# A graph layer on one core: the last pieces' x half of W1 is computed at the start, and VectorE adds it back late

## The chip, the cores and the metric

The kernel runs on one core of a Trainium2 chip. The metric is the device time of one execution in microseconds (us). The launch has one core, so nothing else shares its engines.

## The reference

A graph with 6250 nodes and 106250 edges, 128 numbers (f32) for each. `dst`, sorted, names the node that each edge ends in.

```python
agg = segment_sum(edge_attr, dst, num_segments=6250)       # 6250 x 128
h   = concatenate([x, agg, u[0] for every node], axis=1)   # 6250 x 272
h   = relu(h @ W1 + b1)                                    # 6250 x 256
out = h @ W2 + b2
y   = x + (out + x)
return (y - mean(y)) / sqrt(var(y) + 1e-5)                 # over the 128 columns
```

## The kernel before

**Groups and batches.** The edges are cut into 70 groups of 1536 (the last has 266). A group is four windows of 384 edges, and the destinations of a window span fewer than 32 nodes. SyncE loads the groups in order into a ring of 12 slots, 768 KB each (`load_group`, line 276). Two groups make a batch up to group 59; from group 60 on each group is a batch by itself. There are 40 batches; number 30 is the first single one (`late_step`).

For each batch b the engines do this. VectorE compares the local destinations with 0..31 and so makes the one-hot matrices (`make_onehot`, line 594) and a 128-wide placing matrix (`make_place`, lines 603 and 608). TensorE multiplies edges by one-hots (`sum_batch`, line 845), which gives sums by node. ScalarE copies these out of PSUM (`copy_batch`, line 441). TensorE turns and places them (`turn_batch`, line 867), and VectorE adds them to the turned table `agg_t` (`add_batch`, line 630). Step b of TensorE is `sum_batch(b)`, then `turn_batch(b - 1)`, then work on pieces.

**Pieces.** The nodes are cut into ten pieces of 512 (0 to 9, the last of them `LAST`) and the late ones A, B, C_ of 256, D, E of 128 and REST of 106. A piece n can go on once all groups up to `complete_at[n]` are added. Its work: x is turned on TensorE (`turn_x`, line 882) and copied by ScalarE (line 453); `sum_hidden_x` (line 900) multiplies it by the x rows of W1, and `sum_hidden_a` (line 907) adds `agg_t` times the other rows in the same PSUM bank; ScalarE applies bias and Relu (`relu`, line 466); `sum_out` (line 920) multiplies by W2; VectorE forms y and its moments (`moments`: lines 641, 647, 652), ScalarE takes the root (`root`, line 473), and VectorE normalizes (`normalize`: lines 656, 660). GpSimd adds half of b2 to x beforehand (line 402).

**The start.** SyncE loads part of `dst`, group 0, the rest of `dst`, then the groups, with the x of a piece after every sixth group; the late pieces' x stands between groups 53 and 54 (lines 296 to 303). VectorE makes local destinations, TensorE turns them (line 834), ScalarE copies them (line 429). Only then can the first one-hots be made.

**The end.** The order on each engine from batch 30 on is written out by hand. On VectorE it is the following, where `step(b)` is one-hots for batch b + 2, placing for b + 1, then the add of batch b - 1:

```python
            b = late_step
            step(b)
            step(b + 1)
            moments(LAST)
            step(b + 2)
            normalize(LAST)
            step(b + 3)
            moments(A)
```

On TensorE it is `sum_batch`, `turn_batch` of the batch before, and then `sum_out(LAST)` at step 30; hidden A at 31; out A and hidden x of B at 32; hidden a of B at 33; out B at 34; hidden x of C_ at 35; hidden x of D and hidden a of C_ at 36; out C_ and hidden a of D at 37; out D and hidden x of E at 38; hidden x of REST at 39; at last hidden a of E and REST and their outs.

Of the kernel before, what the change touches and what calls it, by code (L numbers as in the profile page):

```python
# [13 lines left out]
R = 3  # L14
# [8 lines left out]
BUFFERS = 3  # L23
# [5 lines left out]
GEN_TILES = 10  # L29


def gnn_resnorm_kernel(nc: bass.Bass, x: bass.AP, dst: bass.AP, edges: bass.AP, u: bass.AP,
# [16 lines left out]
    rest_rows, rest_tiles = divmod(rest_edges, R)  # L49
    agg_cols = (n_nodes // BLOCK + 1) * BLOCK  # L50
    assert 0 < rest_edges <= EDGES_WIN and 0 < rest_tiles and rest_rows < ROWS
# [20 lines left out]
    complete_at = [6, 12, 18, 24, 30, 36, 40, 46, 52, 58, 60, 63, 66, 67, 69, n_grp]  # L72
    assert len(complete_at) == n_pieces
    steady = 6
    assert all(complete_at[n] * BLOCK == pieces[n + 1][0] * IT for n in range(steady))
    late_groups = [(complete_at[n], pieces[n + 1][0]) for n in range(steady, n_pieces - 1)]


    single0 = 60
# [7 lines left out]
    hidden_step = [batch_first.index(complete_at[n]) for n in range(n_big)]  # L87
    out_step = [b + 1 for b in hidden_step]
    turn_x_step = [1] + out_step[:n_big - 1]

    x_parts = [(n,) for n in range(n_big)] + [(A, B), (C_, D, E), (REST,)]
    x_load_at = {1: 0} | {IT * n: n for n in range(1, n_big)}
    x_late_at = 53
# [7 lines left out]
    with ExitStack() as ctx:  # L103
# [27 lines left out]
        late_base = sb("late_base", [P, len(late_groups)])  # L131
# [20 lines left out]
        x_t_late = sb("x_t_late", [P, n_nodes - late0])  # L152
        hid_t = sb("hid_t", [P, 2, m_chunks, BLOCK])
# [25 lines left out]

        def out_bank(n):  # L180
            return xt_ps if n >= n_big and n % 2 == 0 else out_ps
# [3 lines left out]
        bases_landed = sem("bases_landed")  # L185
        weights_landed = sem("weights_landed")
# [26 lines left out]
        x_t_ready = sem("x_t_ready")  # L213
        hidden_summed = sem("hidden_summed")
# [35 lines left out]
        n_weights = 7  # L250
# [6 lines left out]
        CHECK0 = 2  # L257
        WORST_STEP = CHECK0 + 4
        assert out_step[0] < WORST_STEP < out_step[1]

# [5 lines left out]
        def _(sp):  # L266
            dst_full = dst[0:full_grp * EDGES_GRP].rearrange("(g c e) -> g c e", c=C, e=EDGES_WIN)
            sp.dma_start(dst_rows[0:64], dst_full[0:64]).then_inc(dst_landed, 16)

            def load_group(g):  # L270
# [9 lines left out]
                src = edges[g * EDGES_GRP:g * EDGES_GRP + rest_rows * R, :].rearrange("(p r) f -> p (r f)", r=R)  # L280
                to = edge_ring[0:rest_rows, slot, 0:R].rearrange("p r f -> p (r f)")
# [3 lines left out]
                sp.dma_start(edge_ring[rest_rows:rest_rows + 1, slot, 0:rest_tiles],  # L285
# [3 lines left out]
            def load_x(n):  # L289
                node0, p, j = pieces[n]  # L290
                sp.dma_start(rows(n, x_all).rearrange("p j f -> p (j f)"),  # L291
                             x[node0:node0 + p * j, :].rearrange("(p j) f -> p (j f)", j=j)
                             ).then_inc(x_landed[n], 16)

            def load_x_late():
                sp.dma_start(x_all[:, x_slot[A]:x_slot[D]].rearrange("p (n j) f -> p n (j f)", j=J // 2),
                             x[late0:rest0 - 2 * P, :].rearrange("(n p j) f -> p n (j f)", p=P, j=J // 2)
                             ).then_inc(x_landed[n_big], 16)
                sp.dma_start(x_all[:, x_slot[D]:x_slot[REST]],
                             x[rest0 - 2 * P:rest0, :].rearrange("(n p) f -> p n f", p=P)  # L300
                             ).then_inc(x_landed[n_big + 1], 16)
                for r0, r1 in ((0, rest_cut), (rest_cut, rest_nodes)):
                    sp.dma_start(x_all[r0:r1, x_slot[REST]], x[rest0 + r0:rest0 + r1, :]
                                 ).then_inc(x_landed[n_big + 2], 16)

            load_group(0)

            sp.wait_ge(pad_set, 1)
            sp.dma_start(dst_rows[64:full_grp], dst_full[64:full_grp]).then_inc(dst_landed, 16)
            sp.dma_start(dst_rows[full_grp:n_grp, 0, 0:rest_edges],  # L310
                         dst[full_grp * EDGES_GRP:n_edges].rearrange("(o e) -> o e", o=1)).then_inc(dst_landed, 16)
            for g in range(1, n_grp):
# [3 lines left out]
                if g == x_late_at:  # L316
                    load_x_late()
# [88 lines left out]
        def _(act):  # L406
            nc.scalar.preload_act_table(ACT.Sqrt)
            loads = [
                (w1_x[:], w1[0:d, :]),
# [7 lines left out]
            assert len(loads) == n_weights  # L417
            act.dma_start(base_row[0:1, 0:n_grp],
                          dst.rearrange("(o e) -> o e", o=1)[:, 0:n_edges:EDGES_GRP],
                          allow_slow_non_contiguous=True).then_inc(bases_landed, 16)  # L420
            for to, src in loads:
                act.dma_start(to, src, allow_slow_non_contiguous=True).then_inc(weights_landed, 16)

# [8 lines left out]
            last.then_inc(local_t_ready, 1)  # L432

            def copy_batch(b):
# [5 lines left out]
                w = C * WIN if b < n_batch - 1 else WIN  # L440
# [3 lines left out]
            def copy_x_t(k):  # L444
                act.wait_ge(x_turned, k + 1)
                if 2 <= k < n_big:

                    act.wait_ge(hidden_summed, m_chunks * (k - 1))
                at = 0
                for n in x_parts[k]:  # L450
                    node0, p, j = pieces[n]
                    to = x_t[:, k % 2] if k < n_big else x_t_late[:, node0 - late0:node0 - late0 + p * j]
                    last = nc.scalar.copy(to.rearrange("f (p j) -> f j p", j=j),  # L453
                                          xt_ps[:, at:at + p * j].rearrange("f (j p) -> f j p", j=j))
                    at += p * j
                last.then_inc(x_t_ready, 1)

            def relu(n):
                _, p, j = pieces[n]
                for m in range(m_chunks):  # L460

                    act.wait_ge(hidden_summed, m_chunks * n + (m + 1 if n < n_big else m_chunks))
                    if n >= 2 and m == 0:

                        act.wait_ge(out_summed, n - 1)
                    nc.scalar.activation(hid_t[:, n % 2, m, 0:p * j].rearrange("h (j p) -> h j p", j=j),  # L466
# [598 lines left out]
```

## Time and profile before

| | |
|---|---|
| median of 3 runs | 185.4 us (185.38 to 186.12) |
| profiled execution: its own time | 185.73 us |
| profiled execution: span, first to last instruction | 184.0 us |
| TensorE busy | 154.1 us, 84% |
| VectorE busy | 115.4 us, 63% |
| ScalarE busy | 51.5 us, 28% |
| GpSimd busy | 25.4 us, 14% |
| moved | 62.07 MB |

The span is cut into stages by what ends the waits: the stretch until the last pair of groups has landed, the stretch in which the single groups and late pieces are worked off, and the tail of the last piece. An engine's share over the whole span doesn't say which of them it bounds.

### The profile page before, as it was taken

Reading aid. Unit: us, or ns where it says so; the run is one execution under the profiler, and the core shown is the slowest. Engines: PE = TensorE matmul, PEld = TensorE weight load, DVE = VectorE, ACT = ScalarE, POOL = GpSimd, SP = SyncE. Lnnn points to the kernel's source line nnn. Section 1 sums busy time; section 2 is a strip of 40 time slices with the busy share of each in tenths; the row PEclk is TensorE's granted clock in tenths of the full one; section 3 lists DMA queues with packets and bytes.
Section 4 is the critical chain, followed back from the end, with each engine's and each line's share of the span. In section 5 each row is a group of like instructions: output and inputs, shape, how many; then the busy total and the mean of one; then the engine's idle time right before and its main releaser. Section 6 shows DMA issues by size and latency. Waiting matters only on the chain.

```text
span 184.0 us, 5378 instructions
## 1 busy us (share of the span) xinstructions
PE 154.1 (84%) x2195; PEld 113.9 (62%) x2195; DVE 115.4 (63%) x369; ACT 51.5 (28%) x110; POOL 25.4 (14%) x29
## 2 busy tenths in 40 slices
PE   0056979979979979969979999899889799899970
PEld 0046855955955956845846858467458568677850
DVE  6847499568376385485495466954933745877371
ACT  2021233223323313313313343133133241233230
POOL 7800030110200200200200204002003230000000
PEclk9999999999999999999999999999999999999997
DMA  5999999999999999999999999999999999998011
GB/s 119 315 352 373 374 375 373 371 373 374 374 374 373 375 372 373 376 372 373 374 373 374 375 373 374 375 373 360 363 374 374 371 374 370 367 398 303 11 43 33
DMA packets 42196, 62.07 MB, mean 337 GB/s; under 512 B 1975, under 2 KB 39541, under 8 KB 42170
## 3 DMA queue, kind: packets, MB, share of 16 engines
q1 hardware_dynamic: 41046, 61.23, 95.0%
q10 hardware_dynamic: 1124, 0.48, 1.2%
q8 instruction: 18, 0.29, 0.7%
q14 instruction: 8, 0.07, 0.1%
HBM read 58.50 MB, written 3.20 MB: 335 GB/s over the span
## 4 chain that ended last, share of the span: by engine, by line
PE 44%; DMA 39%; SPq 8%; DVE 4%; ACT 1%; issue 1%; DVEq 0%
DMA edge_ring<-in_edge_attr_dram 37%; PE sum_ps L845 17%; PE turn_ps L867 7%; PE hid_ps L907 6%; PE hid_ps L900 6%; PE out_ps L920 5%; SPq L276 4%; SPq L291 3%; DMA base_row<-in_dst_dram 2%; DVE bases L568 2%; PE xt_ps L920 1%; PE xt_ps L882 1%; DVE local_rows L576 1%; ACT local_t L429 1%; PE xt_ps L834 1%
## 5 line engine op out<-in xcount | busy, mean ns | idle before, releaser
L845 PE MATMUL sum_ps<-edge_ring,onehot 128*32 128x128 f32 x1662 | 58.5, 284 | 13.0 <-DMA edge_ring<-in_edge_attr_dram 10.8
L845 PEld LDWEIGHTS sum_ps<-edge_ring,onehot 128*32 128x32 f32 x1662 | 45.2, 113 | 27.9 <-DMA edge_ring<-in_edge_attr_dram 13.3
L630 DVE TENSOR_TENSOR agg_t<-agg_t,turn_ps 128x128 f32 x70 | 20.2, 288 | 56.7 <-PE turn_ps L867 52.6
L594 DVE TENSOR_TENSOR onehot<-iota,local_t 128x768 f32<-128x768 f32 (+1 forms) x40 | 33.6, 843 | 3.0 <-ACT local_t L429 2.4
L402 POOL TENSOR_TENSOR x_all<-x_all,half_b 128x512 f32<-128x512 f32 (+3 forms) x16 | 17.7, 1115 | 127.4 <-PE xt_ps L882 127.4
L466 ACT ACTIVATE hid_t<-hid_ps,bias 128x512 f32<-128x512 f32 (+3 forms) x32 | 18.1, 584 | 37.1 <-PE hid_ps L907 37.1
L867 PE MATMUL turn_ps<-place,sums 128*128 128x128 f32 (+1 forms) x140 | 26.5, 306 | 0.0
L907 PE MATMUL hid_ps<-agg_t,w_a 128*128 128x512 f32 (+3 forms) x64 | 24.1, 500 | 0.6 <-DVE agg_t L630 0.5
L867 PEld LDWEIGHTS turn_ps<-place,sums 128*128 128x128 f32 (+1 forms) x140 | 18.9, 192 | 8.0 <-issue 7.9
L920 PE MATMUL out_ps<-w_sb,hid_t 128*128 128x128 f32 (+1 forms) x176 | 21.9, 275 | 0.0
L441 ACT COPY sums<-sum_ps 128x256 f32<-128x256 f32 (+2 forms) x40 | 13.6, 341 | 25.9 <-PE sum_ps L845 25.9
L920 PEld LDWEIGHTS out_ps<-w_sb,hid_t 128*128 128x128 f32 (+1 forms) x176 | 20.7, 192 | 0.2 <-ACT hid_t L466 0.2
L900 PE MATMUL hid_ps<-x_t,w_x 128*128 128x512 f32 x40 | 18.9, 594 | 0.0
L907 PEld LDWEIGHTS hid_ps<-agg_t,w_a 128*128 128x128 f32 x64 | 11.2, 190 | 11.3 <-issue 6.4
L453 ACT COPY x_t<-xt_ps 128x512 f32<-128x512 f32 x10 | 11.6, 1158 | 22.4 <-PE xt_ps L882 22.4
L660 DVE TENSOR_SCALAR x_all<-x_all,mean_var,rstd 128x128 f32<-128x128 f32 (+1 forms) x49 | 13.9, 342 | 0.5
L608 DVE TENSOR_TENSOR place<-iota,rel_cols 128x256 f32<-128x256 f32 x30 | 13.6, 454 | 0.0
L473 ACT ACTIVATE std<-mean_var,eps_col 128x4 f32<-128x4 f32 (+3 forms) x16 | 4.6, 294 | 27.5 <-DVE mean_var L652 27.5
L647 DVE BATCH_NORM_STATS2 stats<-x_all 128x6 f32<-128x128 f32 (+1 forms) x49 | 11.0, 281 | 0.5
L900 PEld LDWEIGHTS hid_ps<-x_t,w_x 128*128 128x128 f32 x40 | 6.8, 191 | 4.8 <-issue 4.8
L641 DVE SCALAR_TENSOR_TENSOR x_all<-x_all,out_ps 128x512 f32<-128x512 f32 (+3 forms) x13 | 7.8, 599 | 0.4 <-PE out_ps L920 0.4
L826 PE MATMUL out_ps<-ident,rel 70*4 70x70 f32 x1 | 0.3, 277 | 9.1 <-DVE rel L574 9.1
(64 smaller groups left out, 73.0 us busy)
## 6 DMA issues: line engine op xcount, KB each, us to landing
edge_ring<-in_edge_attr_dram SPq DMA_DIRECT2D x69, 768.0 KB, 12.1
x_all<-in_x_dram SPq DMA_DIRECT2D x10, 256.0 KB, 10.5
out_dram<-x_all SPq DMA_DIRECT2D x1, 2304.0 KB
dst_rows<-in_dst_dram SPq DMA_DIRECT2D x1, 384.0 KB
x_all<-in_x_dram SPq DMA_DIRECT2D x1, 384.0 KB, 11.1
out_dram<-x_all SPq DMA_DIRECT2D x3, 128.0 KB
out_dram<-x_all SPq DMA_DIRECT2D x1, 256.0 KB
w_x<-in_L_gnn_W_dram ACTq DMA_DIRECT2D x1, 128.0 KB, 5.9
```

The source lines that it names most:

```text
L402: nc.gpsimd.tensor_tensor(xn, xn, half_b2[0:p].unsqueeze(1).broadcast_to([p, j, d]), ALU.add).then_inc(xb_ready, 1)
L441: nc.scalar.copy(sums[0:w, b % 2, 0:k], sum_ps[b % 2][0:w, 0:k * d].rearrange("s (k f) -> s k f", k=k)).then_inc(batch_copied, 1)
L466: nc.scalar.activation(hid_t[:, n % 2, m, 0:p * j].rearrange("h (j p) -> h j p", j=j), hidden_bank(n, m).rearrange("h (p j) -> h j p", j=j ...
L594: nc.vector.tensor_tensor(onehot[0:ROWS, b % BUFFERS, 0:k * TILES], cols, loc, ALU.is_equal).then_inc(onehot_ready, 1)
L608: nc.vector.tensor_tensor(place[:, b % BUFFERS, 0:k], cols, at, ALU.is_equal).then_inc(place_ready, 1)
L630: nc.vector.tensor_tensor(to, to, turn_ps[b % 2][:, i * SPAN:(i + 1) * SPAN], ALU.add).then_inc(group_added, 1)
L660: last = nc.vector.tensor_scalar(y_n[:, jj], y_n[:, jj], moments_n[:, jj, 0:1], rstd_n[:, jj:jj + 1], ALU.subtract, ALU.mult)
L845: last = nc.tensor.matmul(bank[c * WIN:(c + 1) * WIN], onehot[0:p, b % BUFFERS, i * TILES + c * R + r], edge_ring[0:p, slot, c * R + r], s ...
L867: last = nc.tensor.matmul(turn_ps[b % 2][:, i * SPAN:(i + 1) * SPAN], sums[0:w, b % 2, i], place[0:w, b % BUFFERS, i], start=True, stop=True)
L900: nc.tensor.matmul(hidden_bank(n, m), w1_x[:, m * P:(m + 1) * P], src, start=(m == 0 or not late), stop=False, skip_group_check=late)
L907: nc.tensor.matmul(hidden_bank(n, m), w1_a[:, m * P:(m + 1) * P], agg_t[:, node0:node0 + p * j], start=False, stop=True, skip_group_check= ...
L920: last = nc.tensor.matmul(out_bank(n)[0:p, jj * d:(jj + 1) * d], hid_t[:, n % 2, m, jj * p:(jj + 1) * p], w2_sb[:, m], start=(m == 0), sto ...
```

## The change

The x of the late pieces is loaded right after `dst` and ahead of group 0. TensorE turns it and multiplies it by the x rows of W1 while the destinations are prepared (9 transposes and 6 matmuls); ScalarE copies the turned x and then the products to SBUF (`x_hid_late`). At the end `sum_hidden_a` of a late piece stands alone in its bank, VectorE adds the stored product to it (`add_x_hidden`), and ScalarE applies Relu to the sum. `BUFFERS` goes from 3 to 6; VectorE's step adds first and makes one-hots up to five batches ahead. `moments` and `normalize` come a step earlier each, except that out of LAST and the late pieces keep TensorE's old steps. The x rows of W1 are loaded first on ScalarE's queue. Three x loads (pieces 7, 8, 9) move two groups forward. `BLOCK / IT` for the least base is replaced by one entry per piece (15 small operations and one reduction in place of 10 and 9). The code for a last group of several windows changes nothing at this size.

```diff
-BUFFERS = 3
+BUFFERS = 6
+AHEAD = 5
+    hidden_step[A] = max(hidden_step[A], late_step + 1)
     out_step = [b + 1 for b in hidden_step]
+    made_by = [min(b + 3 + sum(hidden_step[n] <= b for n in range(AHEAD - 2)), n_batch) for b in range(n_batch)]
...
-            load_group(0)
             sp.wait_ge(pad_set, 1)
...
-            for g in range(1, n_grp):
+            load_x_late()
+            for g in range(n_grp):
                 load_group(g)
                 if g in x_load_at:
                     load_x(x_load_at[g])
-                if g == x_late_at:
-                    load_x_late()
...
+            for k in range(n_late):
+                copy_x_late(k)
+            keep_x_hidden(0)
...
             last.then_inc(local_t_ready, 1)
+            for k in range(1, n_late):
+                keep_x_hidden(k)
...
+            def add_x_hidden(n):
+                dve.wait_ge(hidden_summed, m_chunks * (n + 1))
+                if n == A:
+                    dve.wait_ge(late_x_ready, n_late)
+                for m in range(m_chunks):
+                    xh = x_hid_late[:, m, late_cols_of(n)]
+                    nc.vector.tensor_tensor(xh, hidden_bank(n, m), xh, ALU.add).then_inc(late_added, 1)
...
-                if b + 2 < n_batch:
-                    make_onehot(b + 2)
-                if b + 1 < n_batch:
-                    make_place(b + 1)
                 if b > 0:
                     add_batch(b - 1)
+                for m in range(made_by[b - 1] if b > 0 else 2, made_by[b]):
+                    make_onehot(m)
+                    make_place(m - 1)
+                if b == n_batch - AHEAD - 1:
+                    make_place(n_batch - 1)
...
+            for b in range(late_step, n_batch):
+                step(b)
+                for n in range(LAST, n_pieces):
+                    if out_step[n] + 1 == b:
+                        normalize(n)
+                for n in range(LAST, n_pieces):
+                    if out_step[n] == b:
                         moments(n)
+                for n in range(A, E):
+                    if hidden_step[n] == b:
+                        add_x_hidden(n)
...
+            pe.wait_ge(consts_ready, 3)
+            for k in range(n_late):
+                turn_x_late(k)
+            pe.wait_ge(w1_x_landed, 16)
+            sum_x_late(0)
...
+            pe.wait_ge(x_t_ready, n_late)
+            for k in range(1, n_late):
+                sum_x_late(k)
...
             pe.wait_ge(local_t_ready, 1)
+            pe.wait_ge(late_x_ready, n_late)
...
+            for b in range(late_step, n_batch):
+                sum_batch(b)
+                turn_batch(b - 1)
+                for n in range(LAST, E):
+                    if out_step[n] == b:
+                        sum_out(n)
+                for n in range(A, E):
+                    if hidden_step[n] == b:
+                        sum_hidden_a(n)
```

The new steps of TensorE are 31, 33, 36, 37 for hidden a of A, B, C_, D, and one more for their outs. ScalarE's step is `copy_batch`, `root` of the piece whose out was a step before, then `relu`.

## Rows read from the trace of the kernel before

**Rows 1.** The page: what the DMA engines moved, in 40 slices of 4.6 us.

```profile
GB/s 119 315 352 373 374 375 373 371 373 374 374 374 373 375 372 373 376 372 373 374 373 374 375 373 374 375 373 360 363 374 374 371 374 370 367 398 303 11 43 33
```

**Rows 2.** Windows: length, busy us of each engine (instructions), granted clock, DMA share, GB/s.

```profile
2.00:5.00 3.00, 0.00 (x0) 0.00 (x0) 2.38 (x22) 0.09 (x1) 2.86 (x5) 1.00 0.90 218
...
15.00:118.00 103.00, 94.90 (x1451) 70.36 (x1452) 67.26 (x198) 29.66 (x56) 11.71 (x8) 1.00 1.06 374
```

**Rows 3.** The page's groups: the sums over edges, busy, mean ns, idle before.

```profile
L845 PE MATMUL sum_ps<-edge_ring,onehot 128*32 128x128 f32 x1662 | 58.5, 284 | 13.0 <-DMA edge_ring<-in_edge_attr_dram 10.8
```

**Rows 4.** Timeline of SyncE's queue at the start: start, duration, instruction.

```profile
1.45 0.56 SPq L276 DMA_DIRECT2D edge_ring<-in_edge_attr_dram  x1
...
2.67 0.22 SPq L310 DMA_DIRECT2D dst_rows<-in_dst_dram  x1
```

**Rows 5.** The chain that ended last, from group 59's load on: start, duration, what.

```profile
132.54 11.96 DMA edge_ring<-in_edge_attr_dram
...
149.49 0.44 PE xt_ps L882 x4
149.92 0.79 PE sum_ps L845 x24
...
151.36 1.79 PE out_ps L920 x16
153.14 0.09 PE xt_ps L882
...
154.03 0.42 PE turn_ps L867 x2
154.45 0.87 PE hid_ps L900 x4
...
160.83 1.13 PE hid_ps L907 x4
...
173.17 0.45 PE hid_ps L900 x4
...
177.74 0.70 PE out_ps L920 x4
```

**Rows 6.** Timeline of VectorE, steps 31 to 33.

```profile
154.78 0.68 DVE L641 SCALAR_TENSOR_TENSOR x_all<-x_all,out_ps 128x512 f32<-128x512 f32 x1
...
156.70 0.53 DVE L594 TENSOR_TENSOR onehot<-iota,local_t 128x384 f32<-128x384 f32 x1
...
157.52 0.29 DVE L630 TENSOR_TENSOR agg_t<-agg_t,turn_ps 128x128 f32 x1
157.73 0.17 DVE L656 RECIPROCAL rstd<-std 128x4 f32<-128x4 f32 x1
...
158.97 0.55 DVE L594 TENSOR_TENSOR onehot<-iota,local_t 128x384 f32<-128x384 f32 x1
...
160.70 0.41 DVE L641 SCALAR_TENSOR_TENSOR x_all<-x_all,xt_ps 128x256 f32<-128x256 f32 x1
...
161.83 0.53 DVE L594 TENSOR_TENSOR onehot<-iota,local_t 128x384 f32<-128x384 f32 x1
```

**Rows 7.** Timeline of ScalarE: Relu of piece A, both halves.

```profile
156.21 0.84 ACT L466 ACTIVATE hid_t<-hid_ps,bias 128x256 f32<-128x256 f32 x2 [1.85 <-PE hid_ps L907]
```

**Rows 8.** Timeline of all engines from 5 to 24 us.

```profile
5.33 3.35 DVE L568 TENSOR_SCALAR bases<-base_row 1x72 int32<-1x72 int32 x1 [0.59 <-DMA base_row<-in_dst_dram]
...
8.88 1.75 DVE L576 TENSOR_TENSOR local_rows<-dst_rows,base_f 70x1536 f32<-70x1536 int32 x1
...
15.40 5.35 PE L845 MATMUL sum_ps<-edge_ring,onehot 128*32 128x128 f32 x96 [2.23 <-issue]
...
17.29 0.42 DVE L608 TENSOR_TENSOR place<-iota,rel_cols 128x256 f32<-128x256 f32 x1
...
22.94 1.57 POOL L402 TENSOR_TENSOR x_all<-x_all,half_b 128x512 f32<-128x512 f32 x1 [14.31 <-PE xt_ps L882]
23.30 1.50 DVE L608 TENSOR_TENSOR place<-iota,rel_cols 128x256 f32<-128x256 f32 x1
```

More of the change, by code:

```diff
@@ L69, in gnn_resnorm_kernel @@
     x_slots = sum(p[2] for p in pieces)
-    complete_at = [6, 12, 18, 24, 30, 36, 40, 46, 52, 58, 60, 63, 66, 67, 69, n_grp]
+    complete_at = COMPLETE_AT + [n_grp]
     assert len(complete_at) == n_pieces
[L74 to L79, printed above, removed]
+    least_at = [(complete_at[n], pieces[n + 1][0]) for n in range(n_pieces - 1)]
+    single0 = complete_at[LAST] + PAIR
     batch_first = list(range(0, single0, PAIR)) + list(range(single0, n_grp)) + [n_grp]
@@ L178, in hidden_bank, with late_cols_of @@
             return hid_ps[n % 2][:, m * half:m * half + p * j]
+        def late_cols_of(n):
+            node0, p, j = pieces[n]
+            return slice(node0 - late0, node0 - late0 + p * j)
+        late_turned = [turn_ps[0], turn_ps[1], sum_ps[0]]
+        late_hidden = [[sum_ps[1][:, :], hid_ps[1][:, :]], [turn_ps[0][:, :], turn_ps[1][:, :]],
+                       [sum_ps[0][:, m * late_cols[2]:(m + 1) * late_cols[2]] for m in range(m_chunks)]]
         def out_bank(n):
@@ L822, in _, with turn_x_late, sum_x_late @@
         def _(pe):
+            def turn_x_late(k):
+                pe.wait_ge(x_landed[k], 32 if k == n_late - 1 else 16)
+                if k == 1:
+                    pe.wait_ge(x_landed[0], 16)
+                at = 0
+                for n in late_parts[k]:
+                    _, p, j = pieces[n]
+                    for jj in range(j):
+                        last = nc.tensor.transpose(late_turned[k][:, at:at + p], x_all[0:p, x_slot[n] + jj],
+                                                   ident[0:p, 0:p])
+                        at += p
+                last.then_inc(x_turned, 1)
+            def sum_x_late(k):
+                pe.wait_ge(x_t_ready, n_late if k == n_late - 1 else k + 1)
+                for m in range(m_chunks):
+                    last = nc.tensor.matmul(late_hidden[k][m], w1_x[:, m * P:(m + 1) * P],
+                                            x_t_late[:, late_col[k]:late_col[k] + late_cols[k]], start=True, stop=True)
+                last.then_inc(late_x_summed, 1)
+            pe.wait_ge(consts_ready, 3)
[3 more added lines that the diff above has]
+            sum_x_late(0)
             pe.wait_ge(consts_ready, 4)
@@ L884, in turn_x, with sum_hidden_a @@
                 last.then_inc(x_turned, 1)
             def sum_hidden_x(n):
+                pe.wait_ge(x_t_ready, n_late + n + 1)
+                if n > 0:
+                    pe.wait_ge(hidden_ready, m_chunks * n)
+                for m in range(m_chunks):
+                    nc.tensor.matmul(hidden_bank(n, m), w1_x[:, m * P:(m + 1) * P], x_t[:, n % 2],
+                                     start=True, stop=False)
+            def sum_hidden_a(n):
                 node0, p, j = pieces[n]
@@ L888, in sum_hidden_x @@
                 late = n >= n_big
-                if not late:
-                    pe.wait_ge(x_t_ready, n + 1)
-                    if n > 0:
-                        pe.wait_ge(hidden_ready, m_chunks * n)
-                else:
-                    pe.wait_ge(x_t_ready, len(x_parts))
-                    pe.wait_ge(hidden_ready, m_chunks * max(n - 1, n_big))
-                for m in range(m_chunks):
-                    src = x_t_late[:, node0 - late0:node0 - late0 + p * j] if late else x_t[:, n % 2]
-                    nc.tensor.matmul(hidden_bank(n, m), w1_x[:, m * P:(m + 1) * P], src,
-                                     start=(m == 0 or not late), stop=False, skip_group_check=late)
```

289 lines of the change are left out of this document (121 added, 168 removed).

## The prediction

> **What bounds the kernel now.** I read the page's slices first, then windows, then the chain of waits, then the engines' timelines at both ends. The slices [rows 1] show about 374 GB/s in nearly every slice from the fourth on; the long window [rows 2] says the same, with a DMA share at its ceiling. TensorE meanwhile sat idle for 10.8 us before the sums over edges because an edge load had not landed [rows 3]. So up to group 59 the kernel is bound by the loads. The chain shows where this ends: group 59 lands at 144.50 (132.54 + 11.96) [rows 5]. Behind it the chain is TensorE almost without a gap until the last out matmul ends at 178.44 [rows 5]. Is this second stretch also near the loads' limit? A group of 786432 bytes at 374 GB/s takes 2.10 us, so by estimate group 68 lands at 144.5 + 9 x 2.10 = 163.4 and the short group 69 soon after. TensorE sums them several us later than that, so there TensorE is the bound, with room below it. From 178.44 to the end of the span, 5.6 us, it is the last piece's moments, root, normalization and store; the change leaves that tail as it is.
>
> **Removed from TensorE's path.** From the end of hidden 9 (149.49) to 178.44 are 28.95 us. Out of them go the transposes of late x that lie on the chain, 0.44 and 0.09, and six pairs of hidden x matmuls: three of 256 columns at 0.86 to 0.87 (one row stands for three) and three of 128 or 106 columns at 0.43 to 0.45 (again one for three) [rows 5]. That is 0.53 + 2.60 + 1.33 = 4.46 us. If nothing took their place, the span would be 179.5.
>
> **What takes their place.** Relu of a late piece now waits for VectorE's two adds, and these stand last in VectorE's step, behind a batch's add, a one-hot, a placing matrix, a normalization and moments. I price them by start-to-start times. Moments of 512 nodes take 154.78 to 156.70 = 1.92; normalization takes 157.73 to 158.97 = 1.24; an add of a batch 0.21 (157.52 to 157.73); a one-hot and placing about 0.46 + 0.29 together 0.75; moments of 256 nodes 160.70 to 161.83 = 1.13 [rows 6]. The new add of 128x256 from PSUM isn't in the trace. Its nearest rows are the 0.41 of the 256-wide operation with a PSUM input and the 0.29 of the 128-wide add [rows 6]; I take 0.41, the second ending 0.33 after the first; 0.29 each is the lower bound, 0.47 each an upper one (half of the 0.84 of ScalarE's pair [rows 7]).
>
> Piece A. TensorE: sum of group 60 ends 150.28, turn 150.92, out LAST 152.71 (0.79, 0.64, 1.79 [rows 5]), sum 61 153.50, turn 153.92 (0.42), hidden a of A 154.79 (0.87). VectorE: moments(LAST) can start at 152.74 and hold it to 154.66; then the batch's add to 154.87, one-hot and placing to 155.62, normalize(LAST) to 156.86. Only then the two adds for A, ready since 154.8: they end at 157.27 and 157.60. Relu's second half (0.47, half of the 0.84 [rows 7]) ends at 158.15. TensorE is through with sum 62 and turn at 156.00 and stands. A matmul group after a stand also costs more: 1.13 instead of 0.87 (160.83 against 154.45) [rows 5]. So out A ends at about 159.38 instead of 156.89. This one place gives back 2.5 us. Behind out A are queued sum 63 and everything after it.
>
> The other pieces by the same reckoning. Piece B: its adds start at 162.40, behind normalize(A), out B ends at 164.92, 0.6 later than by TensorE's work alone. The wait of hidden a of C_ for the add of batch 35, which the hidden x of D used to fill, costs 0.4 more than before. Out C_ loses 0.4, out D 0.8. At the end, from the last turn to the end of out REST, the adds for E and REST make 3.05 us of what was 2.79, 0.3 more. Together 2.5 + 0.6 + 0.4 + 0.4 + 0.8 + 0.3 = 5.0 us against 4.46 removed: **+0.5 us**. Bounds: with adds of 0.29 each and no extra cost after a stand the sum is 3.2, so -1.3; with 0.47 each and six more register loads before the add of batch 30 (a row for one is not at hand; I allow up to 0.5 in all) it is +1.5. Making one-hots ahead saves VectorE three pairs of 0.75 between steps 35 and 39, where the reckoning already has none.
>
> **The start of the loads.** Group 0 used to be issued at 1.45, right behind the first part of `dst` [rows 4]. Now SyncE first waits for the fill, which is one operation of 1270 columns instead of two, about as long, until about 2.05. Then the rest of `dst` to about 2.67 or 2.9 [rows 4], four x loads at 0.22 to 0.56 each (the spread of the issues in [rows 4]), and group 0 at about 4.3 instead of 1.45. Are the DMA engines idle for it? In front of group 0 there are now 0.58 MB of x that used to come later, 1.55 us at 374 GB/s, and the engines moved only 218 GB/s from 2 to 5 us anyway [rows 2]. The queue has work except between the end of the first `dst` part and the first x bytes. I take 0.4 us lost, with 0 below (W1's x rows, issued first, fill the hole) and 2.8 above (the whole shift of group 0's issue). Every load behind it shifts, group 59 included. On the other side the dips to 360 and 363 in slices 28 and 29, where the small x rows are loaded now [rows 1], are worth (14 + 11) x 4.6 / 374 = 0.3 us, and I let them move to the start with the rows: nothing. The x loads of pieces 7 to 9 move within what lands before group 59: nothing.
>
> **TensorE's start.** The late x work comes at about 6 to 10 us. The prepared destinations don't wait for it until VectorE has finished line 576, at 10.63 [rows 8], which hides it. Then four more matmuls and four copies stand ahead of the first sums, and I put the first sum about 2 us after 15.40 [rows 8]; at most 4. This lies under the 10.8 us in which TensorE waits for loads before 144.5 [rows 3], and group 12's slot is free long before its load: nothing. W1 ahead of `base_row` delays that by a us, under the 3.35 us of line 568, which ended at 8.68 only [rows 8]: nothing. Adding first in each step before step 30 is under the loads too.
>
> GpSimd's additions to late x, now in a row after about 19 us, come beside VectorE's one-hots. The trace has such a meeting: a placing matrix that takes 0.42 by itself took 1.50 beside a GpSimd addition of 1.57 [rows 8]. By about 3.6 us of additions I allow VectorE 3.6 us of delay at most; with the 4 above that is 7.6 us, still under 10.8. The Trainium skill, SBUF — State Buffer, section "Who interferes with whom", says that a VectorE instruction with two SBUF inputs contends with a GpSimd instruction that reads SBUF; by that rule the early additions also hit the one-hots, and the late ones leave the end free. The trace agrees with its 1.50 us.
>
> **Sum.** 0.5 + 0.4 = +0.9: the span goes from 184.0 to 184.9, the profiled execution's own time from 185.73 to 186.6. The median lay 0.33 below that execution, so I forecast 185.4 + 0.9 = **186.3 us**.
>
> **Rivals.**
> 1. VectorE doesn't hold up the late pieces: Relu comes in time, TensorE keeps most of the 4.46 us and loses only the last piece's 0.3 and the 0.4 at C_. 4.46 - 0.7 - 0.4 at the start = 3.4 less, 182.0 us; a partial form, with stalls near the lower bound, gives 184.0. For it: VectorE is busy only 63%. Against it: the written order, in which A's adds come after 3.2 us of moments and normalization. It decides if A's adds start before about 155. Chance 0.24.
> 2. The loads start late: group 0's data shift by the issue, 2.8 instead of 0.4, so 185.4 + 0.5 + 2.8 = 188.7; at half that 187.3. For it: 218 GB/s between 2 and 5 us shows that the queue is not yet full. Against: 0.58 MB stands before it. Decides above 1.1 us of idle DMA. Chance 0.12.
> 3. The early lag isn't absorbed: TensorE has not caught up with the loads when group 59 lands. It takes more than the 10.8 us of idle [rows 3]; at 12 us, the time is 186.3 + 1.2 = 187.5. Against: 7.6 at most by the rows above. Chance 0.04.
> 4. My own case, stalls of 3.9 to 6 us at the end: 0.60, with its own range 185.2 to 187.4.
>
> A change of 0.5%, 0.9 us, is about what a measurement can tell. Faster, below 184.5: most of rival 1, 0.22. Slower, above 186.3: half of my case, rivals 2 and 3, and that makes 0.39. Same: 0.39. The range 183.8 to 187.6 leaves out rival 1's full form and rival 2's.
>
> **What the profile after would show.** Group 59 landing at 144.9, with the GB/s of the slices unchanged but for the first two; the first sum at about 17 to 19; in the chain, at out A, a VectorE and ScalarE piece instead of TensorE alone; VectorE's adds for A starting some 2 us after hidden a of A ended. Wrong would make it: adds for A within 0.5 us of their matmul, or group 59 landing more than a us away from 144.9.

## The result, and the profile after

The changed kernel takes 189.94 us, the median of four runs (188.59 to 191.07), against 185.5 for the kernel before: 1.0225 times as long, with a 95% interval of 1.0188 to 1.0263. I had forecast 186.3, in a range to 187.6. Executions that took over 1.5% more than the fastest of the same kernel are left out of all ratios and intervals, but not of the medians. Its profiled execution took 191.07 with a span of 189.4, against 185.73 and 184.0. The 5.4 us between the spans divide so, each part from a start to an end in both traces:

| stretch | before | after | more |
|---|---|---|---|
| start to the sum of group 59 | 144.55 | 146.68 | 2.1 |
| from there to the end of the last out matmul | 33.89 | 36.97 | 3.1 |
| tail | 5.56 | 5.75 | 0.2 |

**The loads.** The page's GB/s, in slices of 4.7 us, answers to [rows 1]. The first four slices look different (380 follows 311), and the dip of the late x in slices 28 and 29 is gone.

```profile
GB/s 140 307 311 380 373 375 372 374 372 372 375 372 373 375 373 373 374 374 371 376 373 374 370 374 373 370 370 374 376 373 371 372 374 369 400 274 41 0 42 32
```

SyncE's queue at the start answers to [rows 4]: group 0 is issued at 4.85 and not at 1.45, and nothing is issued between 1.40 and 2.29, while SyncE waits for the fill (constants that VectorE writes first, among them into the unused end of `dst_rows`).

```profile
0.82 0.58 SPq L299 DMA_DIRECT2D dst_rows<-in_dst_dram  x1
2.29 0.35 SPq L346 DMA_DIRECT2D dst_rows<-in_dst_dram  x1
...
2.95 0.42 SPq L334 DMA_DIRECT2D x_all<-in_x_dram  x1
...
4.85 0.94 SPq L307 DMA_DIRECT2D edge_ring<-in_edge_attr_dram  x2
```

Windows of 1 us of the changed kernel (columns as in [rows 2]) show two weak stretches, one from 3 to 5 us and one from 10 to 11, where the DMA share is 0.56 only.

```profile
3.00:4.00 1.00, 0.00 (x0) 0.00 (x0) 0.46 (x6) 0.00 (x0) 1.00 (x2) 1.00 0.95 207
4.00:5.00 1.00, 0.00 (x0) 0.00 (x0) 0.00 (x0) 0.00 (x0) 1.00 (x1) 1.00 0.86 165
...
10.00:11.00 1.00, 1.00 (x3) 0.49 (x2) 0.64 (x1) 0.00 (x0) 0.00 (x0) 1.00 0.56 148
```

The sum of group 59 starts 2.1 us later than before, and it waits for its load:

```profile
146.68 0.86 PE L912 MATMUL sum_ps<-edge_ring,onehot 128*32 128x128 f32 x24 [0.43 <-DMA edge_ring<-in_edge_attr_dram]
```

But were bytes lost? One window from 0 to 144.50, of the changed kernel and then of the one before:

```profile
0.00:144.50 144.50, 122.49 (x1793) 88.47 (x1797) 93.76 (x272) 43.52 (x82) 24.40 (x29) 1.00 1.04 361
```

```profile
0.00:144.50 144.50, 120.84 (x1808) 88.81 (x1808) 92.43 (x276) 40.54 (x73) 23.35 (x25) 1.00 1.04 362
```

The difference is 1 GB/s x 144.5 us = 0.14 MB, worth 0.4 us at 374 GB/s (0 to 0.8, as both are rounded). That is my term of 0.4 us, but it is a net figure: the changed kernel differs in more than the place of group 0. The same window of g0_first (experiment 1), which issues group 0 at 1.45 again, reads 363, and so does that of x_before_wait (experiment 12), which issues late x there (the line is that of g0_first):

```profile
0.00:144.50 144.50, 124.55 (x1829) 89.87 (x1833) 91.93 (x280) 44.13 (x84) 24.83 (x29) 1.00 1.05 363
```

So the late issue costs 2 GB/s against these, about 0.8 us (0.4 to 1.2). Whether the early small rows give part of it back is open: of the two kernels that have only them, experiment 4's reads 363 and experiment 10's 362. In the landing of group 59 there are 2.1 us, and bytes alone don't make them.

The trace also keeps, for each load of a group, the times at which its 16 parts landed. TensorE may start only when the last has. For groups 0, 5 and 59, in us (g0_first is experiment 1):

```
          group   first   median   15th     last
before      0      6.79     7.02     7.43     8.03
before      5     20.10    20.35    20.91    20.93
before     59    141.16   143.23   144.39   144.50
after       0      9.94    10.16    11.89    13.05
after       5     21.63    22.13    22.98    24.38
after      59    141.58   142.67   145.24   146.63
g0_first   59    140.96   142.51   144.26   144.38
adds_early  5     21.84    22.61    24.24    25.30
adds_early 59    141.10   144.18   145.81   145.93
filler      5     21.88    22.72    23.48    23.50
filler     59    141.32   143.35   145.56   145.67
```

In the changed kernel the median part of group 59 lands 0.6 us *earlier* than before. The last lands 2.1 us later. It is 2.2 us behind the median at group 5 already, and 4.0 at group 59. This picture is that of one execution. adds_early and filler (experiments 2 and 3) start their loads in the same way, and there the last part of group 59 is 1.8 and 2.3 us behind a median that is itself late. What the three share is a late last part, 145.67 to 146.63. The Trainium skill, DMA: Bandwidth & Descriptors, section "Why a DMA increments its semaphore by 16 and not by 1", says that only the full count means that all data has landed; the trace agrees, by the 146.63 and the sum at 146.68.

**The end.** The chain from hidden 9 on answers to [rows 5]:

```profile
153.05 1.80 PE out_ps L979 x16
154.88 0.70 DVE x_all L670
155.60 0.88 DVE stats L676 x4
...
156.88 0.50 issue
...
157.83 0.47 DVE onehot L623
...
159.13 0.60 DVE x_all L689 x2
159.73 0.34 DVE x_hid_late L700
160.10 0.36 ACT hid_t L523
...
160.54 0.52 ACT hid_t L523
...
161.09 2.08 PE xt_ps L979 x8
163.17 1.38 PE sum_ps L912 x24
```

It leaves TensorE at the end of out LAST and returns at out A, as forecast: VectorE has the moments of LAST, one-hots and the normalization of LAST before the adds for A at 159.65, and Relu comes behind. Two things are new. One is 0.50 of "issue": VectorE reads the bases of the next groups into registers there. The other is out A itself, 2.08 us, and the sums after it, 1.38 instead of 0.79. The windows around it say why (the third number from the right is the granted clock):

```profile
151.62:158.06 6.44, 6.44 (x100) 5.21 (x100) 3.70 (x15) 1.52 (x4) 0.00 (x0) 1.00 1.06 373
158.06:161.09 3.03, 0.07 (x1) 0.00 (x0) 2.99 (x12) 0.99 (x3) 0.00 (x0) 0.98 1.07 366
161.09:163.17 2.08, 2.08 (x12) 1.85 (x16) 0.17 (x1) 0.10 (x1) 0.00 (x0) 0.50 1.05 398
163.17:164.56 1.39, 1.39 (x26) 0.99 (x25) 1.16 (x5) 0.00 (x0) 0.00 (x0) 0.57 1.05 401
```

TensorE works without a gap to 158.06, stands (is idle) for 3.03 us, and then works at a granted clock of 0.50, the 1.2 GHz level; by 164.56 it is back at 1.00. The Trainium skill, TensorE: Matmul & The Clock Gate, section "HAM oscillation — how this bites in real kernels", describes a kernel whose TensorE waits for a load between its matmuls and starts the next ones at half the clock; by that rule the stand costs more than its own length, and the trace agrees with 0.50 right behind it. The longest wait of the kernel before in this stretch is 0.48 us, and my sum, which had a stand of 2.2 us there (156.00 to 158.15), had no term for the clock.

### The profile page after: what moved, and what is told of

Same layout as the page of the kernel before. It is cut to its first block, busy times and chain, and to the rows that moved or that the text cites. A ratio compares the mean times of both kernels' runs of the same rounds, so it can differ in the third digit from the quotient of the medians.

```text
span 189.4 us, 5371 instructions
## 1 busy us (share of the span) xinstructions
PE 155.6 (82%) x2183; PEld 112.4 (59%) x2183; DVE 120.0 (63%) x377; ACT 54.6 (29%) x116; POOL 24.6 (13%) x29
## 4 chain that ended last, share of the span: by engine, by line
PE 37%; DMA 34%; SPq 16%; DVE 6%; ACT 2%; issue 2%; DVEq 0%; ACTq 0%
DMA edge_ring<-in_edge_attr_dram 34%; PE sum_ps L912 13%; SPq L307 8%; SPq L329 6%; PE out_ps L979 6%; PE hid_ps L966 6%; PE turn_ps L934 5%; PE hid_ps L953 5%; PE xt_ps L979 2%; ACT hid_t L523 2%; DVE stats L676 1%; PE xt_ps L944 1%; DVE x_hid_late L700 1%; DVE x_all L689 1%; DVE x_all L670 1%
## 5 line engine op out<-in xcount | busy, mean ns | idle before, releaser
L912 PE MATMUL sum_ps<-edge_ring,onehot 128*32 128x128 f32 x1662 | 57.0, 277 | 14.9 <-DMA edge_ring<-in_edge_attr_dram 13.8
L912 PEld LDWEIGHTS sum_ps<-edge_ring,onehot 128*32 128x32 f32 x1662 | 43.2, 110 | 30.6 <-DMA edge_ring<-in_edge_attr_dram 15.8
L438 POOL TENSOR_TENSOR x_all<-x_all,half_b 128x512 f32<-128x512 f32 (+3 forms) x16 | 17.0, 1078 | 119.1 <-PE xt_ps L944 108.0
L523 ACT ACTIVATE hid_t<-hid_ps,bias 128x512 f32<-128x512 f32 x20 | 13.7, 687 | 29.8 <-PE hid_ps L966 29.8
L523 ACT ACTIVATE hid_t<-x_hid_late,bias 128x256 f32<-128x256 f32 (+2 forms) x12 | 4.8, 453 | 10.9 <-DVE x_hid_late L700 10.9
L868 PE MATMUL turn_ps<-ident,x_all 128*128 128x128 f32 x8 | 1.9, 424 | 7.1 <-DMA x_all<-in_x_dram 7.1
```

Source lines behind the costliest of these rows:

```text
L438: nc.gpsimd.tensor_tensor(xn, xn, half_b2[0:p].unsqueeze(1).broadcast_to([p, j, d]), ALU.add).then_inc(xb_ready, 1)
L912: last = nc.tensor.matmul(bank[c * WIN:(c + 1) * WIN], onehot[0:p, b % BUFFERS, i * TILES + c * R + r], edge_ring[0:p, slot, c * R + r], s ...
```

## The experiments

Where not said otherwise an edit is made to the changed kernel. Ratios are to the kernel before, with a 95% interval; "the end" is the time from the start of group 59's sum to the end of the last out matmul, 33.89 us before and 36.97 after the change. Landings, waits and ends are read from one profiled execution of each kernel. The experiments ran in several series, so the ratios are a safer comparison between them than the medians.

**1. Group 0 first again (g0_first).**

```diff
+            load_group(0)
             sp.wait_ge(pad_set, 1)
...
-            for g in range(n_grp):
+            for g in range(1, n_grp):
```

> The changed kernel with group 0's load issued again ahead of SyncE's wait for the fill; all else as changed. Theory P (the loads start late because group 0 stands behind the wait and the late x): group 59 lands at about 144.9 instead of 146.63, and the span falls by about 1.7 us, to 187.7. Rival Q (the small rows of late x at the start, not group 0's place, cost the loads their 2 us): group 59 lands within 0.5 us of 146.6 and the span stays at 189.4.

Measured: 187.91 us, ratio 1.0103 [1.0052, 1.0153], 2.0 us less than the changed kernel by the medians and 1.2% by the ratios. The sum of group 59 is back at

```profile
144.42 0.86 PE L913 MATMUL sum_ps<-edge_ring,onehot 128*32 128x128 f32 x24 [0.41 <-DMA edge_ring<-in_edge_attr_dram]
```

and the last part of its load at 144.38 (table above). So the place of group 0 in the queue costs about 2 us. In this profiled execution the clock stayed low until about 169 us, longer than in the changed kernel's, so its end of 38.89 is not compared.

**2. The adds for late pieces right behind the batch's add (adds_early).**

```diff
                 if b > 0:
                     add_batch(b - 1)
+                for n in range(A, E):
+                    if hidden_step[n] == b:
+                        add_x_hidden(n)
...
-                for n in range(A, E):
-                    if hidden_step[n] == b:
-                        add_x_hidden(n)
```

> The changed kernel with VectorE's adds of the stored product placed right behind the add of the batch, ahead of one-hots, normalization and moments, in steps 31 to 37. Theory S (TensorE stands because those adds are last in their step): the adds for A start at about 157.7 instead of 159.65, as moments(LAST) still go first; the stand before out A falls from 3.0 to about 1.1 us, those before out B and out C_ nearly vanish, and with the clock not falling the span goes down by 3 to 4 us, to about 186. Rival (Relu or the bank's hand-over is what is late): the stand stays above 2.5 us and the span within 1 us of 189.4.

Measured: 188.02 us, ratio 1.0140 [1.0114, 1.0166]. The end is 34.29 us, 2.7 shorter. TensorE before out A, and at the next place where it waits:

```profile
158.50 1.16 PE L979 MATMUL xt_ps<-w_sb,hid_t 128*128 128x128 f32 x8 [1.08 <-ACT hid_t L523]
...
161.97 1.13 PE L966 MATMUL hid_ps<-agg_t,w_a 128*128 128x256 f32 x4 [1.10 <-DVE agg_t L659]
```

The stand is 1.08 instead of 2.97, and out A takes 1.16. What is late next is the add of batch 32, behind the moments of A: hidden a of B waits 1.10 for it.

**3. TensorE kept at work in the stand (filler).** Three matmuls of 512 columns, of which nobody reads the result, stand ahead of out A.

```diff
+                if b == out_step[A]:
+                    for _ in range(3):
+                        nc.tensor.matmul(hid_ps[1][:], w1_a[:, 0:P], agg_t[:, 0:BLOCK], start=True, stop=True)
```

> The changed kernel with three added 128x128 by 128x512 matmuls in step 32 ahead of out A, into a bank that is written afresh afterwards; they change no result. They fill 2.6 us of the 3.0 us in which TensorE stands. Theory C (about 1.6 us of the loss is the granted clock that falls in the stand): out A's eight row pairs take about 1.1 us instead of 2.08 and the sums after them 0.8 instead of 1.39, the clock stays 1.00 there, and the span falls by about 1.6 us, to 187.8. Rival: the matmuls after the stand are slow for another reason (PSUM or weight reads beside VectorE), they stay slow, and the span is 189.4 or more.

Measured: 188.43 us, ratio 1.0142 [1.0120, 1.0164], 1.5 less than the changed kernel although TensorE does more.

```profile
157.00 2.74 PE L1019 MATMUL hid_ps<-agg_t,w_a 128*128 128x512 f32 x6
...
160.16 1.16 PE L980 MATMUL xt_ps<-w_sb,hid_t 128*128 128x128 f32 x8 [0.41 <-ACT hid_t L524]
```

A matmul has two records here, so x6 are the three. Out A waits for the same Relu but takes 1.16 instead of 2.08. The end is 35.49 us, 1.5 shorter: 0.92 at out A and 0.59 at the sums behind. The cost of the clock is shown to be 1.5 us, apart from the wait itself.

**4. The small rows early, in the kernel before (before_late_x_first).** Late x is loaded behind `dst`, after group 0 and ahead of group 1.

```diff
+            load_x_late()
             for g in range(1, n_grp):
                 load_group(g)
...
-                if g == x_late_at:
-                    load_x_late()
```

> The kernel before with nothing changed but the place of the late x loads: behind dst, ahead of group 1; group 0 is still the second load. Theory P: group 59 lands within 0.4 us of 144.50 and the time is that of before within 0.3%. Rival Q: group 59 lands at 146 or later, and the time is 1.5 to 2 us above that of before.

Measured: 185.66 us, ratio 1.0004 [0.9976, 1.0032]; the last part of group 59 landed at 144.34. Early small rows cost nothing by themselves.

**5. Both repairs (g0_and_adds):** 1 and 2 together.

> Both repairs of the first round in one: group 0's load ahead of the wait, and the adds of the stored product behind the batch's add. If the two causes are separate and add up, group 59 lands at 144.4 and from there to the end it takes what the adds-early kernel took (145.98 to 180.3, 34.3 us), so the last out ends at 178.7 and the span is 184.4, 0.2% above before. Rival: the causes share something (the clock, a queue), and the sum of the repairs is a microsecond or more short of that, 185.5 or above.

Measured: 186.05 us, ratio 1.0014 [0.9980, 1.0048]. The sum of group 59 starts at 144.33, and the end is 34.28 us. The adds early take 1.9 us from g0_first too, as they did from the changed kernel, and group 0 first takes 2.0 from adds_early: by the ratios the adds take 0.85% and 0.89%, group 0 first 1.22% and 1.26%. The two causes add up. What is left of the loss, 0.14%, the interval does not tell from nothing.

**6. Moments and normalization at the steps of before (order_of_before):** experiment 5 with both one step later for LAST to D, and the root behind Relu.

```diff
-                    if out_step[n] + 1 == b:
+                    if out_step[n] + 2 == b:
                         normalize(n)
...
-                    if out_step[n] == b:
+                    if out_step[n] + 1 == b:
                         moments(n)
```

> The kernel with both repairs, and for LAST and the late pieces moments and normalization one step later each, as before the change, with ScalarE's root behind Relu. Theory S: now A's adds wait for nothing but hidden a of A; TensorE stands 0.3 to 0.5 us instead of 1.1 before out A and no longer waits 1.1 us for the add of batch 32; the clock stays. Of the 4.46 us taken from TensorE's path some 3 remain, the last out ends at 176 to 177, the span is 182 to 182.7, and the kernel beats the one before by about 0.8%. Rival (the add on VectorE costs as much as the matmul that it replaces wherever it stands): the span stays at 184 or above.

Measured: 186.80 us, ratio 1.0053 [1.0022, 1.0083]: the expectation failed.

```profile
157.25 1.13 PE L983 MATMUL xt_ps<-w_sb,hid_t 128*128 128x128 f32 x8 [0.99 <-DVE x_all L674]
...
160.75 1.13 PE L970 MATMUL hid_ps<-agg_t,w_a 128*128 128x256 f32 x4 [1.16 <-DVE agg_t L663]
```

Out A no longer waits for Relu but for VectorE's read of out LAST (`x_all`, line 674), which the moments begin with: up to piece A, `sum_out(n)` waits for the y of piece n - 1. Hidden a of B now waits behind the normalization of LAST. I had overlooked that the moments, too, have someone waiting on TensorE. These waits only replace those of experiment 5: up to the end of out C_ both take the same (26.82 and 26.68 us from group 59's sum). The end is 35.75 us against 34.28, and the other 1.3 us lie behind out C_: hidden a of REST waits 0.81 us for the add of the last batch, and at a granted clock of 0.50 from 178 on the last two outs take 1.22 and 1.18 us, where the changed kernel has 0.71 and 0.69.

**7. VectorE's step as before (old_step):** experiment 1 with one-hots two batches ahead, placing one ahead, then the add.

```diff
-                if b > 0:
-                    add_batch(b - 1)
-                for m in range(made_by[b - 1] if b > 0 else 2, made_by[b]):
-                    make_onehot(m)
-                    make_place(m - 1)
+                if b + 2 < n_batch:
+                    make_onehot(b + 2)
+                if b + 1 < n_batch:
+                    make_place(b + 1)
+                if b > 0:
+                    add_batch(b - 1)
```

> The changed kernel with group 0 first, and VectorE's step as before: one-hots two batches ahead and placing one ahead, both in front of the batch's add (still six buffers). Up to group 59 nothing should change (144.4 landing), because loads cover it. At the end one-hots and placing now stand in steps 35 to 37 as well, and the batch's add comes 0.75 us later in every step, so hidden a of B and C_ wait longer: by theory S the span is 0.5 to 2 us above that of the kernel with group 0 first (185.2 to 187). Rival (adding first and working ahead is worth nothing): the same time within 0.4 us.

Measured: 189.29 us, ratio 1.0191 [1.0126, 1.0255], 1.4 more than g0_first, though the two intervals overlap. Hidden a of C_ waits 1.30 for the add of its batch, in the changed kernel 0.48. The stand before out A is 2.31 here, and out A takes 1.16:

```profile
159.22 1.16 PE L979 MATMUL xt_ps<-w_sb,hid_t 128*128 128x128 f32 x8 [2.31 <-ACT hid_t L524]
```

The filler kernel has the change's order at the same granted clock of 1.00 and is the one to compare. Out A starts 13.76 us behind group 59's sum here and 14.44 there; from there to the last out it is 22.29 here and 21.05 there. So adding first costs 0.7 us before out A and gives 1.2 behind it: a gain of 0.6 us, which the two losses hide.

**8. The register reads a step earlier (bases_ahead):** experiment 5, with the bases for groups 60 and 66 read one step ahead of the one that needs them.

```diff
+                for g in (60, 66):
+                    if b == batch_first.index(g):
+                        loaded[g] = load_bases(g // IT)
```

> The kernel with both repairs (group 0 first, adds early), and VectorE reads the window bases of groups 60 to 65 and 66 to 69 from SBUF into its registers a step ahead, while it waits for TensorE anyway, not at the add of batch 30 and 36. Theory R (the 0.5 us without an instruction ahead of the add of batch 30 are those register reads): the 0.5 us vanish from VectorE's path, the stand before out A falls from 1.1 to about 0.6, and the span goes from 184.0 to 183.5. Rival (the gap is a wait or a pipeline effect of the moments before it): it stays, and so does the span.

Measured: 185.20 us, ratio 0.9985 [0.9968, 1.0001]. The add of batch 30 starts 0.30 after the start of the second operation of the moments, 1.04 in the changed kernel; out A starts 11.74 behind group 59's sum, 12.52 in experiment 5. That is 0.8 us on TensorE, as theory R said. Only 0.3 of it reaches the last out (the end is 33.99 against 34.28), since hidden a of B still waits 1.10 for the add of its batch. The ratios say 0.5 us, and their intervals overlap.

**9. Moments only behind the next add (moments_after_adds):** experiment 8, with the moments of A, B and C_ moved to the steps 33, 36 and 38 and part of those of D to the tail. ScalarE's roots move with them; that part of the edit is not shown.

```diff
+    moments_step = {LAST: out_step[LAST], A: out_step[A] + 1, B: out_step[B] + 2, C_: out_step[C_] + 1}
...
-                for n in range(LAST, n_pieces):
-                    if out_step[n] + 1 == b:
-                        normalize(n)
-                for n in range(LAST, n_pieces):
-                    if out_step[n] == b:
-                        moments(n)
+                for n, m in moments_step.items():
+                    if m + 1 == b:
+                        normalize(n)
+                    if m == b:
+                        moments(n)
```

> The bases-ahead kernel, and the moments of A, B, C_ and D moved behind the add of the batch and the adds of the stored product that TensorE waits for next (steps 33, 36, 38 and the tail; those of LAST stay in step 30). Theory S: each hidden a and each out of a late piece then waits only for the shortest chain from the matmul before it, 0.5 us at hidden a of B and C_, 0.3 to 0.7 at each out; the last out ends at about 176.5 instead of 178.6, and the span is 181.8 to 182.5, 0.8 to 1.2% below before. Rival (ScalarE or TensorE's own waits take it over): the span stays at 183 or above.

Measured: 184.92 us, ratio 0.9958 [0.9940, 0.9977]: 0.4% less than the kernel before, and the whole interval is below 1. The end is 32.53 us, 1.4 shorter than before the change. TensorE from out A on:

```profile
156.81 1.16 PE L986 MATMUL xt_ps<-w_sb,hid_t 128*128 128x128 f32 x8 [0.29 <-ACT hid_t L525]
...
159.66 1.13 PE L973 MATMUL hid_ps<-agg_t,w_a 128*128 128x256 f32 x4 [0.48 <-DVE agg_t L664]
```

It still waits, 0.3 before each out and 0.5 before each hidden, but nowhere longer. The last out ends at 177.60 and not at 176.5, and the span, 183.1, is above what I expected. Of the 1.1 us, 0.7 come from group 59, whose last part landed at 145.03 (144.29 in experiment 5) with the median part at 142.34; the other 0.4 lie in the end.

**10. Late x turned early, but its product at the end (before_turned_early):** the kernel before, with only loading, turning and copying of late x moved to the start.

```diff
+            load_x_late()
             for g in range(1, n_grp):
...
-                if b == late_step - 2:
-                    turn_x(n_big)
-                if b == late_step - 1:
-                    turn_x(n_big + 1)
```

> The kernel before with late x loaded behind dst and turned and copied at the start; its multiplication by W1 stays on TensorE at the end. This is the half of the change that puts nothing on VectorE. Theory: 0.53 us of transposes leave TensorE's path at the end and nothing takes their place; loads as before; the span is 183.3 to 183.5, 0.2 to 0.3% below before. Rival (the early work delays the first sums enough to matter, or the loads): the time is that of before or above.

Measured: 185.33 us, ratio 0.9985 [0.9960, 1.0009]; the end is 33.37 us, 0.52 shorter: the 0.53 of transposes, and nothing is given back for it since no new operation of VectorE stands on the path. In the time 0.3% is within the interval.

**11 and 12. What makes the last part late (g0_behind_dst, x_before_wait).** One issues group 0 between the rest of `dst` and late x; the other issues late x ahead of the wait for the fill, and group 0 behind `dst`.

```diff
+            load_group(0)
             load_x_late()
-            for g in range(n_grp):
+            for g in range(1, n_grp):
```

```diff
+            load_x_late()
             sp.wait_ge(pad_set, 1)
...
-            load_x_late()
             for g in range(n_grp):
```

> The changed kernel, but with group 0 issued between the rest of dst and the late x, so at about 2.9 us and not at 4.85. The last of a load's 16 parts sets its landing: in the changed kernel the middle part of group 59 landed at 142.67, earlier than the 143.23 before, and only the last part was late, 146.63. Theory S (one part falls behind because the small late x rows are the first large thing in the queue, ahead of any group): the last part is back, group 59's sum starts at 144.4 to 144.8, and the time falls by about 2 us against the changed kernel, to near that of g0_first, 187.9. Theory I (what counts is how late group 0 is issued): 2.9 instead of 1.45 keeps some 1.0 to 1.4 us of the loss, so the sum starts at 145.4 to 145.9 and the time is about 189.

> The changed kernel, but with the late x issued right behind the first part of dst, ahead of the wait for the fill and of the rest of dst; group 0 then follows at about 4.2 us. Late x still stands ahead of every group, and the queue no longer stands still before it. Theory S (late x ahead of any group lets one part fall behind): group 59's sum starts at 146 to 147 as in the changed kernel, with a spread of 3 to 4 us between its middle and its last part, and the time stays near 189.9. Theory I (the late issue and the stand of the queue before it): the stand is gone and most of the bytes start 1.4 us earlier, so the sum starts at 144.6 to 145.3 and the time is 188 to 188.6.

Measured: with group 0 at 2.95, ahead of late x, the last part of group 59 still lands at 146.67 (median part 142.83). With late x at 1.45 and group 0 at 4.13 only, it lands at 145.21.

```profile
2.95 0.42 SPq L307 DMA_DIRECT2D edge_ring<-in_edge_attr_dram  x1
...
146.71 0.86 PE L913 MATMUL sum_ps<-edge_ring,onehot 128*32 128x128 f32 x24 [0.39 <-DMA edge_ring<-in_edge_attr_dram]
```

```profile
1.45 0.56 SPq L334 DMA_DIRECT2D x_all<-in_x_dram  x1
...
4.13 0.97 SPq L307 DMA_DIRECT2D edge_ring<-in_edge_attr_dram  x2
...
145.25 0.86 PE L912 MATMUL sum_ps<-edge_ring,onehot 128*32 128x128 f32 x24 [1.15 <-DMA edge_ring<-in_edge_attr_dram]
```

Theory S fell by x_before_wait: there late x stands ahead of every group, and group 59 still lands at 145.21. Its time, 188.71 us, ratio 1.0150 [1.0118, 1.0183], is 1.2 less than the changed kernel's. Theory I had its size right (144.6 to 145.3 expected). For g0_behind_dst it was too small (145.4 to 145.9 expected), and this kernel is not settled: its four executions took 187.42 to 192.86, too far apart for a ratio. The landing was read in the longest; the shortest is near what theory S had forecast (187.9).

Over all kernels the picture is this. In the ten with something large issued at 1.45, before SyncE waits for the fill, the last part of group 59 landed at 144.29 to 145.56, and the window from 0 to 144.50 shows 362 to 364 GB/s. In the four without, it landed at 145.67 to 146.67, with 361 GB/s. Whether it is the wait or only the later issue (2.95 for 1.45) that counts was not tested.

## Why the prediction was wrong

**The start of the loads: failed.** I took 0.4 us, from the bytes that the engines would not move. Against the kernel before the windows show just that, against the same kernel with group 0 first 0.8 (0.4 to 1.2). But the landing of a load is that of its last part, for which I had no term. Group 59 came 2.13 us late and not 0.4; group 0 first gives 2.0 back, in two pairs of kernels. This is rival 2 in size (2.8, or 1.4 at half; chance 0.12), though in the changed kernel's trace the median part did not shift with the issue, as it would have by its mechanism. The measurement meets my own mark for a failed step, a landing more than 1 us from 144.9. What stays open: why the last part comes so late, which DMA engine carries it, and how much of it is the scatter between executions. With group 0 first the last part of group 59 landed between 144.29 and 145.56 in six kernels; in three kernels with the changed kernel's start it was 145.67 to 146.63, 1.2 us later on average, which is less than the 2.0 of the times.

**Piece A gives back 2.5: right mechanism, too small.** Moments of LAST, one-hots and normalization stand ahead of the adds, in my order, and an add pair took 0.75 (I had 0.74). From the end of hidden 9 to the end of out A I had 9.89 us, and it took 11.55. Of the 1.66 more, 0.92 is out A at the lower clock (2.08 for 1.16, filler) and 0.50 the register reads, which I had left for the upper bound; the 0.24 left is not shown, though without the reads out A came 0.78 earlier (bases_ahead), not 0.50. My own stand of 2.2 us would have been near old_step's 2.31, behind which out A took 1.16; with the reads it became 2.97. The sums behind out A cost another 0.59 by the clock.

**The other pieces: right.** From out A to out B the chain took 6.12 us for 5.54, and the difference is those slow sums; from out B to out C_ 6.69 for 6.53; from there to the end of out REST 7.68 for 7.49. So the second stretch is 2.6 us above my +0.5, by 1.66 + 0.58 + 0.16 + 0.19.

**Removed, 4.46 us: right.** Those matmuls are gone from TensorE's path, and once the adds, register reads and moments no longer stand in the way 1.4 us of them stay gone (moments_after_adds).

**The chances.** Half of my case with rivals 2 and 3 is 0.30 + 0.12 + 0.04 = 0.46, not the 0.39 that I gave for a slower kernel.

**TensorE's start: right.** The first sum began at 17.55 (17 to 19 forecast), and a placing matrix beside GpSimd's late additions took 1.91, [rows 8] 1.50. None of it reached group 59, whose sum waited for its load. Rival 3 didn't happen, nor did rival 1: A's adds started at 159.65, 2.8 us after hidden a of A.

## What to carry to other kernels

Before work is moved to an engine that takes it in order, list what stands ahead of it in that step and what the waiting engine does meanwhile: a stand of 3 us on TensorE cost 1.5 us more through the clock. Keep a large load at the head of a saturated queue, ahead of its first wait: here that was worth 2 us. Where a stream of loads is the bound, count landings by their last part; nearly equal bytes don't make equal landings.

## What the runs showed of the hardware that I had not expected

- In all four kernels with a stand of 2.97 or 2.98 us before out A, it took 2.07 to 2.08 us; with stands of 2.31, 1.08 and 0.41 it took 1.16. In the changed kernel the clock was back at 1.00 by 164.56, in g0_first only at about 169, some 10 us behind the stand.
- In the changed kernel's execution the last of the 16 parts of a load landed 2.2 to 4.2 us behind the median part in every one of the groups 0 to 59, while the slices from the fourth to its landing moved 370 to 380 GB/s. In the kernel before it was 0.6 to 1.9.
- The register reads of one set of bases held VectorE for 0.50 us, and reading them a step earlier let out A start 0.78 us earlier.
